# Attention with a squared-softplus weight: the maximum in two halves, and output copies on VectorE

## The reference

```
scores = jnp.einsum('bhqd,bhkd->bhqk', q, k) * hs ** (-0.5)
p = jax.nn.softplus(scores)
p = p * p
causal = jnp.tril(jnp.ones((t, t), dtype=p.dtype))
p = p * causal
attn = p / (jnp.sum(p, axis=-1, keepdims=True) + 1e-09)
out = jnp.einsum('bhqk,bhkd->bhqd', attn, v)
```

## Time and profile before

| | |
|---|---|
| median of 3 runs | 2152.83 us (2152.83 to 2156.41) |
| the profiled execution | 2155.49 us, its span 2153.7 us |
| attention phase | from 368 to 991 us of the span |
| busy over the whole span | PE 1726.9, DVE 1493.2, ACT 1148.2, POOL 881.0 us |
| exponential L1067 | 288 times, 1024 ns each |
| logarithm L1071 | 288 times, 1053 ns each |
| maximum L1104 | 288 times, 1218 ns each |
| square L1150 on GpSimd | 240 times, 1894 ns each |
| granted TensorE clock, mean | 0.936 of full speed; 0.99 in attention |

### The profile page before, as it was taken

One profiled execution on the slowest core, in us unless ns is written; L12 is line 12 of the kernel. 1 busy time (PEld: TensorE's weight loads), 2 busy tenths in 40 slices (PEclk: granted clock), 3 DMA queues, 4 the chain that ended last, 5 costly groups with the idle time before them and its releaser, 6 DMA issues. The chain is left out here.

```text
span 2153.7 us, 30865 instructions
## 1 busy us (share of the span) xinstructions
PE 1726.9 (80%) x9712; PEld 1156.7 (54%) x9712; DVE 1493.2 (69%) x2872; ACT 1148.2 (53%) x1624; POOL 881.0 (41%) x605
## 2 busy tenths in 40 slices
PE   4998484777787777778799679996787887859998
PEld 3886373222222222225688557774565665647776
DVE  4555883666766767765555678876688888767886
ACT  2332343999999999995232222212666666652221
POOL 0003222777777777772002431112555555451111
PEclk9999687999999999999899879997899889989999
DMA  4000137325244352410000010000111111100000
GB/s 136 0 0 10 54 121 126 50 44 74 39 62 56 40 77 39 60 19 0 11 0 15 15 35 0 0 0 25 40 40 39 39 39 39 40 20 11 20 19 30
DMA packets 53046, 80.15 MB, mean 37 GB/s; under 512 B 7440, under 2 KB 29040, under 8 KB 52976
## 3 DMA queue, kind: packets, MB, share of 16 engines
q1 hardware_dynamic: 50160, 76.67, 17.6%
q10 hardware_dynamic: 2816, 2.60, 0.6%
HBM read 62.34 MB, written 16.91 MB: 37 GB/s over the span
## 5 line engine op out<-in xcount | busy, mean ns | idle before, releaser
L1150 POOL TENSOR_TENSOR att_weights<-att_weights 128x1024 f32<-128x1024 f32 x240 | 451.9, 1894 | 177.3 <-DVE att_weights L1104 176.8
L1104 DVE SCALAR_TENSOR_TENSOR att_weights<-att_weights,ps 128x1024 f32<-128x1024 f32 x288 | 350.8, 1218 | 190.8 <-ACT att_weights L1071 190.7
L1067 ACT ACTIVATE att_weights<-ps 128x1024 f32<-128x1024 f32 x288 | 294.8, 1024 | 66.2 <-PE ps L1010 50.4
L1007 PE MATMUL ps<-att_q_stack,att_k_stack 128*128 128x512 bf16 (+3 forms) x768 | 198.3, 335 | 155.6 <-DVE att_weights L1104 131.4
L1071 ACT ACTIVATE att_weights<-att_weights 128x1024 f32<-128x1024 f32 x288 | 303.3, 1053 | 0.0
L676 DVE SCALAR_TENSOR_TENSOR X<-ps,moe_gsel,X 128x256 f32 (+1 forms) x512 | 246.3, 483 | 71.4 <-PE ps L47 55.7
L1027 PE MATMUL ps<-att_weights,att_v_ones 128*32 128x512 f32 (+3 forms) x1536 | 288.5, 497 | 1.6 <-POOL att_weights L1150 1.5
L1007 PEld LDWEIGHTS ps<-att_q_stack,att_k_stack 128*128 128x128 bf16 x768 | 66.3, 98 | 358.6 <-DVE att_weights L1104 311.3
L47 PE MATMUL ps<-w_experts_hi,moe_xh 128*128 128x512 f32 x512 | 206.0, 402 | 0.0
L47 PE MATMUL ps<-w_experts_hi,moe_xl 128*128 128x512 f32 x512 | 203.4, 397 | 0.0
L47 PE MATMUL ps<-w_experts_lo,moe_xh 128*128 128x512 f32 x512 | 202.2, 395 | 0.0
(11 more groups left out here) (256 smaller groups left out, 4095.2 us busy)
## 6 DMA issues: line engine op xcount, KB each, us to landing
att_q_stack<-qk_parts SPq DMA_DIRECT2D x128, 128.0 KB, 5.0
ssm_lb<-decays SPq DMA_DIRECT2D x32, 512.0 KB, 3.5
att_k_stack<-qk_parts SPq DMA_DIRECT2D x120, 128.0 KB, 8.5
qk_parts<-qkv_part SPq DMA_DIRECT2D x32, 384.0 KB, 2.5
out<-X SPq DMA_DIRECT2D x8, 512.0 KB, 2.9
X<-in_x SPq DMA_DIRECT2D x3, 1024.0 KB, 5.2
load_raw<-in_ffn_w SPq DMA_DIRECT2D x8, 256.0 KB, 5.8
ffn_raw<-in_moe_w SPq DMA_DIRECT2D x8, 256.0 KB, 2.7
```

What stands on the lines that cost most here:

```text
L1007: ins = pe.matmul(scores(u)[:, t, c:c + w], SK[:, s, h, kj * P:(kj + 1) * P], SQ[:, s, h, q:q + w], start=True, stop=not diagonal)
L1067: act.activation(Wt[:, u % WU], scores(u), ACT.Exp).then_inc(exp_done, 1)
L1104: dve.scalar_tensor_tensor(out=wt, in0=wt, scalar=LIMIT, in1=scores(u), op0=ALU.min, op1=ALU.max)\
L1150: pool.tensor_tensor(Wt[:, u % WU], Wt[:, u % WU], Wt[:, u % WU], ALU.mult).then_inc(sq_pool, 1)
```

## The change

VectorE's maximum of a unit becomes two instructions, one for each half of the slot (one PSUM bank each), and each raises `max_done`, which thus counts two a unit. TensorE waits for half `t` of unit u-3 just before its matmuls into half `t`; all other waits for the maximum ask for both halves. The copy of an output from PSUM to SBUF moves from ScalarE's list to VectorE's: a `tensor_copy` behind the maximum (and square, where there is one) of unit end+7.

```diff
--- before.py
+++ after.py
@@ -999,8 +999,11 @@
                 s, segments = u // PU, pass_units[u % PU]
                 if u % PU == 0:
                     pe.wait_ge(loaded[s], (i + 1) * (16 * 2 * COPIES))
-                pe.wait_ge(max_done, i * NU + u + 1)
+                half = -1
                 for h, kj, t, c, q0 in segments:
+                    if t != half:
+                        half = t
+                        pe.wait_ge(max_done, 2 * (i * NU + u) + t + 1)
                     diagonal = kj // GT == u_block(u)
                     q = u_block(u) * BANK + q0
                     w = segment_width(kj, u_block(u))
@@ -1070,20 +1073,11 @@
                 act.wait_ge(exp_done, i * NU + u + 1)
                 act.activation(Wt[:, u % WU], Wt[:, u % WU], ACT.Ln, bias=1.0).then_inc(ln_done, 1)
 
-            def copy_output(n, i, k):
-
-                act.wait_ge(pv_done, (i + 1) * NS + BLOCK_STEPS[k] + 1)
-                act.wait_ge(o_turned, n + 1)
-                act.activation(oT[:, k % 2], O(k), ACT.Copy).then_inc(oT_done, 1)
-
             def body(i, first=False, last=False):
                 for u in range(NU):
                     if not (last and u == NU - 1):
                         exp(i, u + 1)
                     ln(i, u)
-                    outputs_at(u, BLOCK_UNITS, NU, COPY_LAG, i, first, copy_output)
-                if last:
-                    outputs_left(BLOCK_UNITS, NU, COPY_LAG, i, copy_output)
 
             load(act, 0, 0, (1,))
             act.sem_inc(o_turned, 2)
@@ -1101,11 +1095,18 @@
 
                 wt = Wt[:, u % WU]
                 dve.wait_ge(ln_done, i * NU + u + 1)
-                dve.scalar_tensor_tensor(out=wt, in0=wt, scalar=LIMIT, in1=scores(u), op0=ALU.min, op1=ALU.max)\
-                    .then_inc(max_done, 1)
+                for t in range(2):
+                    dve.scalar_tensor_tensor(out=wt[:, t], in0=wt[:, t], scalar=LIMIT, in1=scores(u)[:, t],
+                                             op0=ALU.min, op1=ALU.max).then_inc(max_done, 1)
                 if by_dve(u):
-                    dve.wait_ge(max_done, SU + i * NU + u + 1)
+                    dve.wait_ge(max_done, 2 * (SU + i * NU + u + 1))
                     dve.tensor_tensor(wt, wt, wt, ALU.mult).then_inc(sq_dve, 1)
+
+            def copy_output(n, i, k):
+
+                dve.wait_ge(pv_done, (i + 1) * NS + BLOCK_STEPS[k] + 1)
+                dve.wait_ge(o_turned, n + 1)
+                dve.tensor_copy(oT[:, k % 2], O(k)).then_inc(oT_done, 1)
 
             def divide_output(n, i, k):
 
@@ -1122,11 +1123,13 @@
             def body(i, first=False, last=False):
                 for u in range(NU):
                     softplus(i, u)
+                    outputs_at(u, BLOCK_UNITS, NU, COPY_LAG, i, first, copy_output)
                     outputs_at(u, BLOCK_UNITS, NU, OUT_LAG, i, first, divide_output)
                 if last:
+                    outputs_left(BLOCK_UNITS, NU, COPY_LAG, i, copy_output)
                     outputs_left(BLOCK_UNITS, NU, OUT_LAG, i, divide_output)
 
-            dve.sem_inc(max_done, SU)
+            dve.sem_inc(max_done, 2 * SU)
             body(0, first=True)
             with dve.Fori(1, BODIES - 1) as i:
                 body(i)
@@ -1146,7 +1149,7 @@
             def body(i, last=False):
                 for u in range(NU):
                     if not by_dve(u):
-                        pool.wait_ge(max_done, SU + i * NU + u + 1)
+                        pool.wait_ge(max_done, 2 * (SU + i * NU + u + 1))
                         pool.tensor_tensor(Wt[:, u % WU], Wt[:, u % WU], Wt[:, u % WU], ALU.mult).then_inc(sq_pool, 1)
                     if u == NU // 3:
                         copy_v(i, 1, (i + 1) * NS)
```

## The result

The changed kernel took 2141.01 us (median of 5 runs, 2138.33 to 2144.26), the kernel before 2153.8 in the same session (5 runs, 2152.83 to 2156.41): ratio 0.9942, interval 0.993 to 0.9953, 12.8 us less. The forecast was 2139.5, faster by more than 0.2%. The profiled execution took 2141.01 with a span of 2139.2.

What follows compares the result with a forecast made beforehand. No engine is full; a ring of dependencies bounds the attention stage. Its section changes sum to −0.83 us per half body, times 16 is −13.3, so 2152.8 becomes 2139.5 us; range 2131 to 2155.

Steps and rivals of the forecast that it cites:

- The ring of two units: Attention stage: maximum, scores, exponential, logarithm, next maximum; 4.00 us before, 3.85 forecast for units of two matmuls.
- The second instruction: VectorE's maximum as two halves takes 1.28 instead of 1.22 us: +0.06 for each maximum on the chain.
- The rival of full cost: VectorE's two half maxima take 1.38 us without overlap: +3 us, 2155; chance 0.15, shared with other losses.
- The early start: TensorE writes half 0 of the scores before the maximum ends, saving 0.22 us (two matmuls) or 0.34 (eight).
- The output copy: Moved from ScalarE to VectorE: 0.68 us long from PSUM, taking a slot of 0.60 there.
- The rival of a short copy: VectorE's output copy takes a slot of only 0.30 or finds a gap: −20 us, 2133; chance 0.15.
- the sum for 20→25: From maximum 20 to maximum 25, with square and copy on VectorE: 9.96 us in all, −0.39.
- half a body: Chain of 18 units, maximum 12 to 30, repeated 16 times: 38.55 us before, −0.83 forecast.
- the copy's slot of +0.60 in 29→30: VectorE's copy behind a square delays maximum 30 by its whole slot; with +0.06 the section grows by 0.66 us.
- ScalarE's 0.48 handed on in 20→25: Between maxima 20 and 25, ScalarE's copy no longer delays the exponential by 0.48 us, mostly handed to VectorE.

Runs made afterwards that it cites:

- the run with one wait: Maximum in halves, but TensorE waits for both halves ahead of the unit; copies on ScalarE, against the kernel before: 2164.6 us, ratio 1.0048.
- the halves alone: The changed kernel with the output copies back on ScalarE: 2132.73 us, against 2155.33 for the kernel before.
- the first copies-only kernel: The kernel before with output copies on VectorE and the whole maximum raising its semaphore by two, one wait of TensorE: 2162.41 us, ratio 1.0037.
- the copies-only kernel with the count by one: The kernel before with only the output copies moved to VectorE, the whole maximum raising its semaphore by one: 2159.27 us, ratio 1.0024.
- the fastest version: The changed kernel with 35 of 36 squares on GpSimd and each output's copy and turn one unit earlier (lags 3, 6, 9): 2109.6 us, ratio 0.9783.

## Why the prediction was right

- *The ring of two units* held: 4.00 before, 3.85 after, each step within 0.01 of the forecast time.
- *The second instruction*: 1.28 for a pair (rows at 716.07 and after), ten times 0.06 by the run with one wait. The rival of full cost, 1.38 a pair and no gain, falls. The prediction backed it with half of what the Trainium skill states ("VectorE: DVE Perf Modes", "The DRAIN you can't avoid"): the same section adds that an instruction that is not held starts earlier. The trace agrees with that addition: the second of a pair starts 0.60 after the first, which lasts 0.68.
- *The early start*: half 1 starts 0.06 after the maximum ends, and the second wait is free (2153.76 against 2153.97 us).
- *The output copy*: 0.683 (0.68 taken). The Trainium skill ("VectorE: DVE Perf Modes", "Why PSUM operands drop a tier") states that a PSUM operand keeps fp32 in the 1× mode, the slowest, and the trace agrees: the copy lasts as long as a maximum of its size (0.681). The rival of a short copy falls. It costs its slot behind the square of unit 29, as said.
- *What the prediction said in two ways*: in words, the copy after maximum 24 fits into VectorE's idle time; in the sum for 20→25 it has its whole slot (1.20 + 0.60). The sum is right: the row at 725.43 is followed by maximum 25 without a gap, and a second copy added 0.59 there.
- *What was off*: half a body gained 0.78 and not 0.83, from 0.01 or 0.02 in six sections; 16 × 0.05 = 0.8 us. The forecast of 2139.5 lay 1.5 below the median, inside the runs' own spread of 6 us. Since every section came out within 0.02, the total is not right by luck.
- *Which part gained*: the forecast had the terms (the copy's slot of +0.60 in 29→30, ScalarE's 0.48 handed on in 20→25), but did not draw from them that the halves alone are the better kernel. The runs say it: 22.6 us by the halves, 8 to 10 of them given back by the copy's move.

## What to carry to other kernels

Where no engine is full, find the ring: write the start times of one instruction kind over a period, name for every section what released each start, and price an edit in those sections only. A step that feeds a ring may be cut in pieces when the consumer can start on the first; the gain is the consumer's work on the first piece, less the producer's extra fixed time, and the added wait cost nothing here. Work moved to an engine with idle time costs its whole slot where it lands on the chain, behind other long instructions of that engine, and when a ring gets shorter, look again at what stood just inside it.

## What the runs showed that I had not expected

In the first copies-only kernel, where one instruction raises the semaphore by two, the maximum starts later after the logarithm: 1.15 us from start to start, against 1.09 before:

```profile
693.54 1.05 ACT L1071 ACTIVATE att_weights<-att_weights 128x1024 f32<-128x1024 f32 x1
...
694.69 1.22 DVE L1095 SCALAR_TENSOR_TENSOR att_weights<-att_weights,ps 128x1024 f32<-128x1024 f32 x1 [0.99 <-ACT att_weights L1071]
```

(693.54 to 694.69; before 688.75 to 689.84.) The trace shows where the 0.06 goes. In this kernel VectorE's wait for the logarithm (L1094) is an instruction of its own on the engine's sequencer (DVEq), once for each of the 288 maxima:

```profile
L1094 DVEq EVENT_SEMAPHORE  x288: 21/21/21, 373.3 to 994.8; - x144
```

A maximum starts 0.07 us after it. In the copies-only kernel with the count by one there is no such row, and the ring is at 3.99. Why the count by two goes with a separate wait stays open.

GpSimd took all but eight of the squares with little harm: in the fastest version it is idle ahead of its 280 squares (1895 ns each) for only 57 us, and still TensorE's product weights wait for it for 22 us in all:

```profile
L1153 POOL TENSOR_TENSOR att_weights<-att_weights 128x1024 f32<-128x1024 f32 x280 | 525.5, 1895 | 57.0 <-DVE att_weights L1099 50.0
```
